# New step lists for the four engines of a fused attention, state-space and mixture-of-experts layer

## What is computed

```
x = layernorm(x + attn(x))        # 16 heads of 8, 4 kv heads, rms norm, rope,
                                  # tanh(s / 50) * 50, causal softmax, w_o
x = layernorm(x + xattn(x, ctx))  # scores against 32 context tokens -> FiLM;
                                  # y = irfft(rfft(x_norm) * rfft(K)); FiLM;
                                  # gelu feed-forward of 512; layernorm
x = layernorm(x + ffn(x))         # 2 shared experts + top 2 of 8 experts
```

## Time and profile before

| what | us |
|---|---|
| median of 3 runs | 549.91 (546.08 to 554.17) |
| the profiled execution | 546.51 |
| its span in the trace | 544.3 |
| PE busy | 438.0 (80% of the span) |
| DVE busy | 332.0 (61%) |
| ACT busy | 324.6 (60%) |
| POOL busy | 229.3 (42%) |

### The profile page before, as it was taken

The page is one execution under the profiler, slowest core; times in us unless marked ns, Lnnn a source line. Parts: engine busy times, 40 slices in busy tenths (PEclk is TensorE's granted clock), DMA queues, the critical chain, the costliest instruction groups (busy, mean ns, idle before and its releaser), DMA issues. The chain is left out here.

```text
span 544.3 us, 9650 instructions
## 1 busy us (share of the span) xinstructions
PE 438.0 (80%) x3369; PEld 316.0 (58%) x3369; DVE 332.0 (61%) x991; ACT 324.6 (60%) x541; POOL 229.3 (42%) x296
## 2 busy tenths in 40 slices
PE   3572575577989979978889899899998799898990
...
PEclk9996756678989989999999999999998999999996
...
DMA packets 39699, 51.40 MB, mean 94 GB/s; under 512 B 8802, under 2 KB 28804, under 8 KB 39652
## 3 DMA queue, kind: packets, MB, share of 16 engines
...
...
HBM read 41.12 MB, written 13.86 MB: 101 GB/s over the span
## 5 line engine op out<-in xcount | busy, mean ns | idle before, releaser
L1107 ACT ACTIVATE probs<-ring_s 128x512 f32<-128x512 f32 x160 | 84.8, 607 | 30.1 <-PE ring_s L784 21.2
L1299 POOL TENSOR_SCALAR_AFFINE_SELECT probs<-probs 128x256 f32<-128x256 f32 (+1 forms) x96 | 50.4, 557 | 103.3 <-ACT probs L1113 103.2
L1160 ACT ACTIVATE g_ring<-ring_s,w_blk 128x128 f32<-128x128 f32 x184 | 52.5, 370 | 48.8 <-PE ring_s L982 48.7
L784 PE MATMUL ring_s<-qT,kT 128*128 128x512 bf16 (+3 forms) x256 | 60.6, 336 | 24.3 <-ACT probs L1107 20.0
L1113 ACT ACTIVATE probs<-probs 128x2560 f32<-128x2560 f32 x32 | 74.6, 2344 | 1.9
L1221 POOL TENSOR_TENSOR rstd<-var_eps,neg_half 128x4 f32<-128x4 f32 x24 | 24.7, 1027 | 102.0 <-DVE var_eps L1547 101.9
L1350 POOL DMA_INDIRECT token_pairs<-y_blk,x_blk x46 | 44.5, 967 | 34.4 <-DVE y_blk L1893 26.0
L801 PE MATMUL bank_o<-probs,vv 128*32 128x128 f32 (+3 forms) x512 | 46.8, 515 | 9.7 <-POOL probs L1299 9.0
L784 PEld LDWEIGHTS ring_s<-qT,kT 128*128 128x128 bf16 x256 | 21.7, 104 | 55.5 <-ACT probs L1107 41.9
L982 PE MATMUL ring_s<-xT_blk,w_blk 128*128 128x128 f32 x368 | 50.3, 281 | 1.7 <-DMA w_blk<-expert_pack 0.9
L982 PEld LDWEIGHTS ring_s<-xT_blk,w_blk 128*128 128x128 f32 x368 | 45.6, 195 | 3.2 <-ACT g_ring L1160 1.5
...
## 6 DMA issues: line engine op xcount, KB each, us to landing
...
```

The lines of the kernel that those rows point to most:

```text
L784: last = mm(bank[:, c:c + w], kT[:, r, p // 2, P * j:P * (j + 1)], qT[:, p, P * j:SEQ], start=True, stop=True)
L1107: f(probs[:, pair % PAIRS_HELD, SEQ * n:SEQ * (n + 1)], ring_s[k % BANKS][:, :], ACT.Tanh, scale=1.0 / (CAP * float(np.sqrt(np.float32(HD) ...
L1160: last = f(g_ring[:, s % RING, P * n:P * (n + 1)], ring_s[s % 2][:, P * n:P * (n + 1)], ACT.Gelu, bias=w_blk[:, k % SLOTS, HID + n:HID + n ...
L1299: last = g.affine_select(out=v, in_=v, compare_op=ALU.is_ge, fill=0.0, base=0, pattern=[[0, v.shape[1]], [1, P]], channel_multiplier=-1)
```

## The change

All four lists are written anew. Every step that stood in a list before stands in it once again, in another place; functions, tiles, buffers, waits and SP's program are the same. PE still does batch after batch, and its list stays as it was from `blkT.26` to the end. The heads of the DVE and the POOL list show the kind of edit:

```diff
--- before.py
+++ after.py
...
-    steps squares.0 rms.0 rope.0 parts.0 v.0 copies.0 states qT.0.1 qT.0.3 vf.0 vf.1 vf.2 qT.0.5 pack angles.0
-    turns.0 vectors vf.3 products.0 amounts.0 angles.1 turns.1 angles.2 turns.2 oT.0 products.1 amounts.1 tokens.0
...
+    steps squares.0 rms.0 rope.0 parts.0 v.0 copies.0 states qT.0.1 squares.1 qT.0.3 vf.0 vf.1 rms.1 vectors pack
+    angles.0 turns.0 vf.2 vf.3 qT.0.5 products.0 amounts.0 angles.1 turns.1 oT.0 angles.2 turns.2 products.1 tokens.0
...
-    mask.0.0 exponents.0 mask.0.1 mask.0.2 exponents.1 mask.0.3 mask.0.4 rope.1.0 mask.0.5 rope.1.1 rope.1.2
...
+    rope.1.0 exponents.0 mask.0.0 mask.0.1 exponents.1 mask.0.2 mask.0.3 mask.0.4 exponents.2 mask.0.5 rope.1.1
```

More of the change, by code:

```diff
@@ L101 @@
 PE_ORDER = steps("""
[L102 to L121, removed]
@@ new lines @@
+    attnT.0 s.1.5.3 s.1.5.4 s.1.6.0 film.0.0 film.0.1 film.0.2 s.1.6.1 film.0.3 s.1.6.2 s.1.6.3 s.1.6.4 s.1.7.0
+    s.1.7.1 PV.6 dft.0.0 dft.0.1 dft.0.2 s.1.7.2 dft.0.3 dft.0.4 s.1.7.3 s.1.7.4 dft.0.5 dft.0.6 dft.0.7 rows.6
+    qT.2.0 qT.2.1 qT.2.2 qT.2.3 qT.2.4 PV.7 conv.0.0 rows.7 s.2.0.0 s.2.0.1 s.2.0.2 yT.1 conv.0.1 s.2.0.3 s.2.0.4
+    proj.1 conv.0.2 s.2.1.0 s.2.1.1 s.2.1.2 conv.0.3 s.2.1.3 conv.0.4 conv.0.5 conv.0.6 x1T.1 conv.0.7 s.2.1.4
+    cross.1 xT.3 s.2.2.0 s.2.2.1 qkv.3 PV.8 s.2.2.2 s.2.2.3 attnT.1 s.2.2.4 s.2.3.0 hT.0 s.2.3.1 s.2.3.2 s.2.3.3
```

171 lines of the change are left out of this document (93 added, 78 removed).

## The result

The changed kernel takes 528.13 us (median of 4 runs, 525.80 to 529.49), the kernel before 551.26 (4 runs, 546.08 to 554.17): ratio 0.959, 95% interval 0.950 to 0.967. That is 23 us, where the prediction had 13. The two profiled executions are 17.0 us apart (spans 527.3 and 544.3); that of the changed kernel took 529.49 us, the longest of its four runs, that of before 546.51, near the shortest of its own.

A forecast was written before the change was run, and what follows sets the result against it. A DVE, ACT, POOL and PE chain was taken to bound batch 0, PE the stages from 127.8 to 382.8 us; 7 + 6.1 + 4.9 - 2 - 3 = 13.0 us off 549.9 gave 537 us, range 527 to 551.

The forecast's parts named there:

- Batch 0, the loss: DVE in batch 0: `squares.1` and `rms.1` ahead of `pack` delay it about 3.9 us, `amounts.0` 5.4 us.
- Batch 0, the gain: End of batch 0: freed DVE and ACT time and later `xT.2` start batch 1 earlier, 6.9 us, taken as 7.
- `xT.2` ... 2.8: ACT ahead of batch 1's first tanh: moving `xT.2` behind seven tanh saves a 1.88 us wait and 0.9 us.
- The hole of `squares.1` and `rms.1`: DVE in batch 0, 74 to 81 us: the two steps' old place becomes free, 6.5 us.
- Batches 1 to 3: Up to 305 us: fewer PE waits for `oT`, `hT.0` and copies just made, 2.5 + 0.6 + 3.0 = 6.1 us saved.
- the 3 us of new waits: PE after batch 0: moved steps whose inputs have less time cost 3 us, a third of the 9.0 us.
- 305 to 382.8 us: PE waits at `gates.1`, `gates.2`, `conv.2.0`, `cross.3`, `hT.2`, `up.2` covered by other work: 4.9 us saved.
- The 2 us for `x_blk`: PE before the first block transpose: waits for loads behind later scatters, 2 us lost, bounds 0 and 6.
- From blkT.16 on: Blocks from 382.8 us to the end: PE's list hardly moves, so 0 us gain or loss.
- The gain stays out: Rival, chance 0.25: later stages take back batch 1's earlier start; about 4 us off, 546 us.
- The sine loop is late: Rival, chance 0.12: DVE's batch 0 ring with ACT delays `PV.1` past about 82; 2 us on top, 552 us.
- The port costs more: Rival, chance 0.11: each POOL `exponents` costs DVE's chain 3.4 us instead of 1.9; 10 off, 540 us.

The follow-up runs named there:

- e4_rms: Changed kernel with `squares.1` and `rms.1` back behind `evacuate.0` on DVE and `rope.1.0` back ahead of `mask.0.5` on POOL: 533.3 us.
- e8_xT2: Changed kernel with `qT.1.5` and `xT.2` on PE and `xT.2` on ACT back ahead of batch 1's first tanh: 532.9 us.
- e5_oT10: Changed kernel with `copies.3` ahead of `oT.10` on DVE again, as before the change: 533.0 us.
- e6_pairs: Changed kernel with four pairs of PE steps joined again (at `gates.1`, `cross.3`, `hT.2`, `gates.2`): 531.0 us.
- e3_tail: Changed kernel with DVE's list from `weigh.21` on in the order of before the change: 523.6 us.
- e7_nat: Changed kernel with DVE's steps in both block groups in the order in which PE issues what they wait for: 521.9 us.
- e1_head: Kernel before with only the first half changed: new lists up to the last steps ahead of batch 1, old order behind: 543.7 us.
- e2_rest: Changed kernel with batch 0 in the order of before, everything behind it new: 537.1 us.

## Why the prediction was right, and where it was off

**Direction and range** held, the range narrowly: 528.1 us is 1.1 us inside its end of 527, and below the 529 to 544 that I gave the forecast itself. By the two profiled executions the sum was 13.0 against 17.0. The medians are 6 us further apart than these, because the execution profiled before was near the shortest of its runs and the one after the longest; the prediction corrected its base for that, not its gain. That the total came this near is in part luck: up to blkT.16 the sum was 10.5 us too small, and behind it it missed a loss of 6.5.

**PE's busy time.** "PE's instructions are the same, so its busy time doesn't shrink" and "I take no gain or loss" from the clock failed. In the four windows where I let an order win only PE's idle time, 5.3 of the 13.1 us came off its busy time.

**Batch 0, the loss.** Right step by step: `rms.1` ended at 41.1, `amounts.0` at 58.8 (58.9 forecast), and `amounts.1` began its last row 5.2 us later than before (78.37 against 73.14). But I had blamed the two early steps for most of it; e4_rms shows 2.0 of it to be theirs.

**Batch 0, the gain.** Mis-sized, 10.3 for 7, and just over my own bound of 10. Right: `PV.1` at 77.6 (77.1), `copies.1` ended at 104.7 (105.7). Too small were two terms. `powers.3` ended at 112.7 for 114.6, and the `qT` row came 6.5 us earlier, not 4.1. And "`xT.2` ... 2.8" is worth 4.6 at the first tanh and 4.7 on the whole (e8_xT2): I took the 1.88 us of the row of before, but with the earlier start ACT would have waited 3.77 for the same transposes. The hole of `squares.1` and `rms.1`, with the loss of their early place taken off, is worth 5.5 to 6 (e4_rms). Each of the two was undone by itself, and together they come to about the 10.3; the smaller terms of my sum had no run of their own. The slow product of `products.0` did not recur: it took 0.69 us (row 54.87), behind POOL's `exponents.0` and no longer beside it, but two rows of `turns.0` pay for it.

**Batches 1 to 3.** 7.6 for 6.1 less a part of the 3 us of new waits. Half of it, 3.8 us, is idle time of PE, which is about what the waits were forecast to give on balance; the other 3.8 came off its busy time, which I had left out. "Of [the 3.5 us] I take 2.5" was too small: undoing it costs 4.8 (e5_oT10), since in the new timeline the wait is 4.46 us and PE ran at 0.50 after it. "The 6.2 us that PE waits for tanh I leave" failed as well: they went to 1.4. PE has other work between the scores now, but no run tests that this is why. New waits came in the size I had feared (`k_parts` 1.6, `x1T` 1.6 where it was 0.8, and 1.4 of scores behind the copy of `xT`).

**305 to 382.8 us.** The pairs were right: 4.9 forecast, 5.5 measured, of which 4.0 are idle time, and joining four of them costs 3.4 (e6_pairs). The 2 us for `x_blk` were wrong. The changed kernel is 17.9 us ahead at the end of the last exponential (287.4 for 305.3). In the times of the kernel before its loads began at 355.3 + 17.9 = 373.2, where I had 375, and PE asked at 377.2, where I had 377.9: 1.8 us earlier than forecast is just in time.

**From blkT.16 on**, "PE's list hardly moves and I take 0" is the step that failed. PE's list hardly moved, but DVE's did: `weigh` steps went ahead of copies that were ready, and `out_end.1` ahead of two copies that PE needed. The stretch took 6.5 us more, with 5.6 us more of waits for DVE in it; 4.3 us come back with DVE's old list (e3_tail) and 7.5 with DVE in PE's order (e7_nat), each uncertain by the 2 to 3 us by which this stretch varies. The 1.9 us that e3_tail leaves open were not traced. Looking at the list of the bounding engine alone hid the one place where the change loses.

**The rivals.** "The gain stays out" fell: e1_head and e2_rest add up to 19.2 of 21.8 us, and e1_head kept its lead of 5.7 us at the first tanh up to the last exponential. "The sine loop is late" fell: `PV.1` at 77.6, not 82. "The port costs more": `turns.0` beside `exponents.0` took 4.2 us for two rows which take 2.0 undisturbed, and `angles.1` beside `exponents.1` 3.4 us for two which take 1.2. So each meeting cost 2.2 to 2.3 us, between my two bounds; the first tanh came 10.3 us earlier all the same. The rows, on DVE and on POOL:

```profile
47.92 2.28 DVE L1505 TENSOR_SCALAR pt<-pa,offs 128x1024 f32<-128x1024 f32 x1
50.24 1.96 DVE L1506 SCALAR_TENSOR_TENSOR pt<-pt,pa 128x1024 f32<-128x1024 f32 x1
```

```profile
46.83 2.82 POOL L1229 TENSOR_TENSOR pr<-pk,index 128x1024 f32<-128x1024 f32 x1 [3.92 <-DVE uf L1498]
49.62 1.50 POOL L1229 TENSOR_TENSOR ue<-pk,index 128x512 f32<-128x512 f32 x1
```

The Trainium skill (SBUF — State Buffer, "Who interferes with whom") would hold DVE for the other's whole instruction. The trace agrees: POOL's first row ends at 49.65, and 0.75 us of DVE's own behind it make 50.40, where the row ends at 50.20; POOL's second ends at 51.12, and 1.23 behind it make 52.35, for 52.20. The three products beside POOL's rows at `rope.1.1` in e4_rms agree to 0.2 us in the same way.
